# Attention passes: 800 tile gathers into a ring and 900 copies from it, in place of 900 gathers

## The chip, the cores and the metric

The kernel runs on one core of one Trainium2 chip. The metric is the device time of one execution in microseconds (us), and the median of the runs is compared.

## The reference, cut to what is computed

A graph of 3125 nodes with 64 features each and 100000 edges sorted by destination goes through two GATv2 attention layers (8 heads, then 4), a layer norm, a neighbour sum with a small dense network, and a second layer norm. The change touches only the two attention layers. One of them is, cut to what matters:

```
xl = (x @ Wl).reshape(N, heads, Dh)
xr = (x @ Wr).reshape(N, heads, Dh)
e = jax.nn.leaky_relu(xl[src] + xr[dst], NEG_SLOPE)
logits = jnp.einsum('ehd,hd->eh', e, att)
m = jax.ops.segment_max(logits, dst, num_segments=n_nodes)
a = jnp.exp(logits - m[dst])
denom = jax.ops.segment_sum(a, dst, num_segments=n_nodes)
out = jax.ops.segment_sum(alpha[:, :, None] * xl[src], dst, num_segments=n_nodes)
```

For every edge the row of its source node (64 floats, 256 bytes) has to be fetched: `x[src]`.

## The kernel before, in words

The edges are cut into 800 **tiles** of 125 edges (`G`, `T`). A **unit** is a tile seen against one window of 32 destination nodes; a tile that crosses a window's border is in two units, so that 800 tiles give 897 units, padded to 900 (`UT`). Twenty units make a **count** (`CU`), and a layer's pass over the edges is 45 counts (`NCH`), each worked in five steps q = 0 to 4 (`NQ`) of four units. The tensors' names begin with L1_ in layer 1 and L2_ in layer 2; the profile leaves the digit out.

In a pass (`edge_pass`) the engines run these streams, in each of which the order is that of the code:

- GpSimd (POOL) issues one indirect DMA per unit (L826, ahead of the pass L533), which gathers 125 rows of `x` from HBM into a buffer of the count, `xs`. There are 6 such buffers in layer 1 and 9 in layer 2. It waits only for the buffer (`v_ready`: the sums of the count that used it last).
- SyncE (SP) loads for each unit its window's node rows, `xw` (L547; 3 buffers). The window's number is read into a register by one load for each unit (L545). Behind the 20 loads it issues in order: the list of windows of the next count (L539), `dlb` of this count (L862), `lim` of the last one (L845), and the store of maxima `me` (L869).
- TensorE (PE) opens each step of a count by turning the four units' rows (L888, function `turn`), which at q = 0 waits for the gathers, for `xw` and for `oht`. Then come the projection (L901), the logits (L910, L913), and for an earlier count the turned maxima and weights (L923) and the weighted sums (L952).
- VectorE (DVE) does everything in one in-order stream. `spread_hot` of count c+1 (L1071), which makes `oht` out of `dlb`, stands in the body of count c at q = 1, n = 3. All of count c's later work on DVE stands behind it.
- ScalarE (ACT) copies, applies relu and exp, and stores the sums.

Layer 1 has four projections of each step, layer 2 has two. Ahead of each pass stands a block that prepares the layer (`prepare_layer`), in layer 2 also one for the neighbour sum's tables (`count_tables`). The blocks are separated by barriers over all engines, and the gathers of the first counts (`AHEAD` = 1 and 4) are issued in them. In the setup (`build_staircase`) the lists are made: `gidx` is the tile of each unit, `srcu` and `src_idx` its 125 source indices.

Of the kernel before, what the change touches and what calls it, by code (L numbers as in the profile page):

```python
# [112 lines left out]
def fixed(c):  # L113
    return Turn(c)
# [94 lines left out]
def build_staircase(nc, k, a, ctx0, x0):  # L209
# [4 lines left out]
    k.src_idx = sbuf(nc, ctx0, "src_idx", [T, UT], I32)  # L214
# [7 lines left out]
    with ExitStack() as ctx:  # L222
# [51 lines left out]
        ps = [psum(nc, ctx, f"ps_setup{i}") for i in range(4)]  # L274
        s = {n: k.setup.enter_context(nc.semaphore("st_" + n)) for n in (
            "load", "iota", "ident0", "ident", "dve", "dve2", "dve3", "store", "transposed", "pad",
            "load2", "sides", "last", "upto2", "node", "keys", "lim", "x_pad", "dloc", "dl0", "row0", "pre", "pre_dma", "below0", "below")}
# [5 lines left out]
        with nc.Block() as block:  # L283
            @block.sync
            def _(sp):
                sp.dma_start(dg[:], a["dst"].rearrange("(p k e) -> p k e", k=KT, e=T)).then_inc(s["load"], 16)
                ld = Dma(sp, s["load2"])
                ld.start(x0[:], a["x"].rearrange("(p t) d -> p t d", t=NT))
                sp.wait_ge(s["pad"], 2)
# [15 lines left out]
                xs.wait()  # L305

# [35 lines left out]
        with nc.Block() as block:  # L342
# [10 lines left out]

            @block.gpsimd
            def _(pool):
                pool.wait_ge(s["dve2"], 2 * NB + 2)
                for b in range(NB):
                    pool.indirect_dma_start(srcu[:, b * T:(b + 1) * T], None, a["src"].rearrange("(g e) -> g e", e=T),
                                            bass.IndirectOffsetOnAxis(gidx[:, b:b + 1], 0)).then_inc(s["gather"], 16)
                    pool.indirect_dma_start(dstu[:, b * T:(b + 1) * T], None, a["dst"].rearrange("(g e) -> g e", e=T),  # L360
                                            bass.IndirectOffsetOnAxis(gidx[:, b:b + 1], 0)).then_inc(s["gather"], 16)
                pool.wait_ge(s["gather"], 32 * NB)
# [22 lines left out]
        with nc.Block() as block:  # L385
            @block.vector
            def _(dve):
# [33 lines left out]
                dve.wait_ge(s["transposed"], 2 * NB)  # L421
                link(dve.tensor_copy(k.src_idx[:, 0:5 * BLK], ps[0][0:T, 0:5 * BLK]))
                link(dve.tensor_copy(k.src_idx[:, 5 * BLK:UT], ps[1][0:T, 0:4 * BLK]))
# [50 lines left out]
            def _(pe):  # L474
                pe.wait_ge(s["dve3"], NB + 2)
                for b in range(NB):
                    c = slice((b % 5) * BLK, (b % 5 + 1) * BLK)
                    pe.transpose(ps[b // 5][0:T, c], srcf[:, b * T:(b + 1) * T],
                                 k.ident[0:BLK, 0:BLK]).then_inc(s["transposed"], 1)
# [47 lines left out]

def fetch_rows(k, pool, lay, u0, u1):  # L530

    for u in range(u0, u1):
        pool.indirect_dma_start(lay.xs[u // CU][:, u % CU, 0:D], None, lay.x_rows,  # L533
# [1523 lines left out]
```

## Time and profile before

| | |
|---|---|
| runs, median of 3 | 4058.42 us (4051.95 to 4059.17) |
| profiled execution, its span | 4048.7 us |
| of it layer 1's pass, from the first turn | 198.5 to about 1810 us |
| layer 2's pass, POOL's gathers | 2085.0 to 3413.3 us |
| PE busy, POOL busy over the span | 3293.6 us, 2796.9 us |
| TensorE's granted clock, mean of the span | 0.90 of full |

The profiled execution's own time is the span from its first to its last instruction; the median of the runs is 9.7 us above it, which lies around the span. A busy time is the sum of instructions' durations. An idle time in square brackets stands before an instruction and names what ended it. DMA-issuing instructions of SP and ACT (SPq, ACTq) and the loads of registers aren't counted as busy.

### The profile page before, as it was taken

How to read it: one execution, taken by the hardware profiler on the slowest of the kernel's cores; microseconds unless marked ns; L12 is line 12 of the kernel's file. 1: busy time of each engine (PE TensorE's matmuls, PEld its weight loads, DVE VectorE, ACT ScalarE, POOL GpSimd, SP SyncE). 2: the span in 40 equal slices, each digit the busy share in tenths (PEclk: the TensorE clock that was granted, in tenths of full speed). 3: DMA queues.
4: the chain of work that ended last, by engine and by line, in shares of the span. 5: the costliest groups of instructions: out<-in, count | busy, mean ns of one | idle time of the engine just before them, and what ended most of it. 6: DMA issues, size and time to landing. Idle time of an engine off the chain costs nothing. (4 is left out here: it accounts for less than half of the span.)

```text
span 4048.7 us, 76266 instructions
## 1 busy us (share of the span) xinstructions
PE 3293.6 (81%) x24199; PEld 2204.4 (54%) x24199; DVE 2807.3 (69%) x6887; ACT 1717.6 (42%) x3696; POOL 2796.9 (69%) x2157
## 2 busy tenths in 40 slices
PE   0399999999999999996339977777777777568986
PEld 0246666666666666674226655554455555346763
DVE  3558888888888888886537755565555555579972
ACT  3254444444444444432215433333333333147861
POOL 4488888888777777505678888888888885537630
PEclk9999999999999999986669988888888888569997
DMA  2233343343333333323114433333333332211210
GB/s 58 51 65 80 86 88 86 86 89 85 80 87 86 86 85 88 75 54 83 48 36 79 91 74 67 68 69 67 67 68 73 69 68 48 52 26 40 44 34 28
DMA packets 607173, 274.68 MB, mean 68 GB/s; under 512 B 445801, under 2 KB 568077, under 8 KB 606260
## 3 DMA queue, kind: packets, MB, share of 16 engines
q1 hardware_dynamic: 261848, 102.14, 11.7%
q0 software_dynamic: 107328, 77.78, 11.1%
q10 hardware_dynamic: 237600, 89.88, 9.1%
q8 instruction: 198, 3.24, 0.3%
q14 instruction: 199, 1.63, 0.1%
HBM read 161.25 MB, written 105.94 MB: 66 GB/s over the span
## 5 line engine op out<-in xcount | busy, mean ns | idle before, releaser
L901 PE MATMUL L_e_ps_z<-L_e_xT,L_w_abs 128*128 128x500 f32 x2700 | 1501.4, 642 | 0.0
L826 POOL DMA_INDIRECT L_e_xs<-in_x_dram,src_idx x880 | 1193.1, 1356 | 335.4 <-issue 261.4
L826 POOL DMA_INDIRECT L_e_xs<-x_d,src_idx x820 | 1079.7, 1317 | 253.3 <-issue 249.8
L952 PEld LDWEIGHTS L_e_ps_v<-L_e_xs,L_e_p 125*128 125x128 f32 x5400 | 860.0, 204 | 628.3 <-issue 569.6
L996 ACT ACTIVATE L_e_rl<-L_e_ps_z 128x500 f32<-128x500 f32 x1350 | 793.0, 587 | 883.0 <-PE L_e_ps_z L901 883.0
L952 PE MATMUL L_e_ps_v<-L_e_xs,L_e_p 125*128 125x65 f32 x5400 | 796.2, 274 | 11.1 <-DVE L_e_acc L1180 9.4
L1180 DVE SCALAR_TENSOR_TENSOR L_e_acc<-L_e_acc,L_e_row,L_e_ps_v 128x130 f32<-128x130 f32 (+1 forms) x1440 | 448.5, 311 | 424.1 <-PE L_e_ps_v L952 281.4
L888 PE MATMUL L_e_ps_x<-ident,L_e_xs 125*64 125x125 f32 x1800 | 288.7, 285 | 310.7 <-DMA L_e_xs<-x_d,src_idx 251.8
L989 ACT ACTIVATE L_e_xT<-L_e_ps_x 128x500 f32<-128x500 f32 x450 | 264.3, 587 | 619.3 <-PE L_e_ps_x L891 590.4
L901 PEld LDWEIGHTS L_e_ps_z<-L_e_xT,L_w_abs 128*128 128x128 f32 x2700 | 427.4, 198 | 77.8 <-issue 24.3
L1163 DVE TENSOR_TENSOR L_e_p<-L_e_ohc,L_e_ae 125x640 f32<-125x640 f32 x540 | 427.1, 818 | 0.0
L888 PEld LDWEIGHTS L_e_ps_x<-ident,L_e_xs 125*64 125x64 f32 x1800 | 188.7, 120 | 354.4 <-DMA L_e_xs<-x_d,src_idx 261.0
L1185 DVE SCALAR_TENSOR_TENSOR L_e_acc<-L_e_acc,L_e_keep,L_e_ps_v 128x65 f32<-128x65 f32 x540 | 134.8, 277 | 314.4 <-PE L_e_ps_v L952 311.9
L1091 DVE SCALAR_TENSOR_TENSOR L_e_f<-L_e_rl,L_sign 128x500 f32<-128x500 f32 x450 | 326.2, 725 | 21.7 <-ACT L_e_rl L996 21.4
L1091 DVE SCALAR_TENSOR_TENSOR L_e_f<-L_e_rl,L_sign,L_e_f 128x500 f32<-128x500 f32 x450 | 329.8, 733 | 4.2 <-ACT L_e_rl L996 0.8
L1655 POOL DMA_INDIRECT g_xs<-x_d,src_idx x168 | 209.1, 1244 | 139.9 <-POOLq L1604 58.9
L1770 ACT ACTIVATE g_cnt<-g_ps_c 125x400 bf16<-125x400 f32 x512 | 257.5, 504 | 63.7 <-PE g_ps_c L1706 54.6
L1800 DVE TENSOR_SCALAR g_ohk<-t_keys_n,t_key_of 125x200 bf16<-125x200 bf16 x1024 | 237.3, 322 | 1.0 <-PE g_ps_c L1706 1.0
L1706 PE MATMUL g_ps_c<-g_ohk,g_ohr 125*128 125x200 bf16 x1024 | 176.7, 255 | 48.2 <-DVE g_ohk L1800 44.5
L1716 PE MATMUL g_ps_s<-g_x,g_cnt 125*128 125x192 bf16 x1600 | 195.8, 248 | 10.4 <-DVE g_sums L1806 10.3
L910 PE MATMUL L_e_ps_l<-L_e_xT,L_w_lin 128*32 128x125 f32 x3600 | 189.9, 283 | 10.5 <-DVE L_e_f L1091 10.5
L891 PE MATMUL L_e_ps_x<-L_e_oht,L_e_xw 96*64 96x125 bf16 x1800 | 193.4, 233 | 0.0
(304 smaller groups left out, 3620.2 us busy)
## 6 DMA issues: line engine op xcount, KB each, us to landing
L_v_d<-L_e_acc ACTq DMA_DIRECT2D x225, 260.0 KB
L_e_dlb<-dloc_d SPq DMA_DIRECT2D x90, 468.8 KB, 4.9
L_v_d<-L_e_acc ACTq DMA_DIRECT2D x225, 130.0 KB
L_e_xw<-x_d SPq DMA_DIRECT2D x1800, 12.0 KB
L_e_xs<-in_x_dram,src_idx POOLq DMA_INDIRECT x900
L_e_xs<-x_d,src_idx POOLq DMA_INDIRECT x900
L_e_lim<-limits_d SPq DMA_DIRECT2D x180, 39.1 KB
L_max_d<-L_e_me SPq DMA_DIRECT2D x45, 78.1 KB
```

The costliest lines, as they stand in the source:

```text
L826: pool.indirect_dma_start(xs[c.slot(XR)][:, n, 0:D], None, lay.x_rows, bass.IndirectOffsetOnAxis(k.src_idx[:, u:u + 1], 0)).then_inc(gath[ ...
L888: pe.transpose(ps[0:D, j * T:(j + 1) * T], xs[r][:, n, 0:D], k.ident[0:T, 0:T])
L901: pe.matmul(ps_z[part % ZR][:, 0:QT], lay.w_abs[:, part * 128:(part + 1) * 128], xT[q][:], start=True, stop=True).then_inc(s["z_ready"], 1)
L952: ins = pe.matmul(ps_v[u // 2 % 2][:, u % 2 * VX + v * XW:u % 2 * VX + (v + 1) * XW], p[st % 3][:, u % NQ, v, :, :].rearrange("e n h -> e ...
L989: act.activation(xT[q][:], ps_x[(c.slot(2) * NQ + q) % 2][:, 0:QT], ACT.Copy).then_inc(s["xT_ready"], 1)
L996: act.activation(rl[n % NE][:], ps_z[part % ZR][:, 0:QT], ACT.Relu, scale=1.0 - SLOPE).then_inc(s["relu_done"], 1)
L1091: dve.scalar_tensor_tensor(out=f[g % 3][:], in0=rl[(C * g + part) % NE][:], scalar=lay.sign[:, part:part + 1], in1=rl[(C * g) % NE][:] if ...
L1163: ins = dve.tensor_tensor(p[n % 3][:, :, v, :, :], ohc[c.slot(2)][:, us, :].unsqueeze(3).to_broadcast([T, NQ, WN, HL]), ae[c.slot(2)][:, u ...
L1180: ins = dve.scalar_tensor_tensor(out=to, in0=prev, scalar=row[c.slot(2)][:, u:u + 1], in1=ps_v[u // 2 % 2][:, u % 2 * VX:(u % 2 + 1) * VX] ...
L1655: pool.indirect_dma_start(xs[p][:, j, :], None, table, bass.IndirectOffsetOnAxis(k.src_idx[:, u:u + 1], 0)).then_inc(gath[p], 16)
L1770: act.activation(cnt[i % CR][:, :, 2 * j:2 * j + 2, :], ps_c[n % 2][0:T, 0:2 * KEYS].rearrange("r (u t n) -> r t u n", u=2, n=EN), ACT.Cop ...
L1800: dve.tensor_scalar(ohk[v % KR][:], keys_n[:], key_of[:, v:v + 1], None, ALU.is_equal).then_inc(s["hot"], 1)
```

## The change

POOL no longer gathers for each unit. It gathers each of the 800 tiles once, in 50 groups of 16 (`NF`, `TF`), into a ring of 64 tiles in SBUF (`TR`; `tiles`). SP copies the rows of each unit out of the ring into `xs` by a plain DMA from SBUF to SBUF, 20 for each count, behind that count's `xw` loads and ahead of its `dlb`. Three semaphores tie the two: `fetched_to` (POOL tells that a group has landed, four gathers into the next group, or at a block's end at once), `copied` (SP tells that a count's copies have landed, once it has issued the next count's `xw` loads), and POOL's wait for `copied` before it overwrites a group's place. The counts that these waits need are worked out in the setup and read into registers. For this input, the groups that the counts 0 to 44 need are 1 to 8 for counts 0 to 7, 10 to 18 for 8 to 16, 20 to 28 for 17 to 25, 30 to 38 for 26 to 34, 40 to 47 for 35 to 42, and 49 for 43 and 44. `xs` has 6 buffers in both layers. The registers of 20 units are now loaded by one instruction (`listed`). `dlb` and `lim` have 2 buffers in layer 1 and 3 in layer 2 (`SLACK`). The setup gathers `srcu` for two of nine blocks only, turns the tiles' indices instead, and stores two more lists.

```diff
+TR = 64
+TF = 16
+NF = G // TF
+RF = TR // TF
+XR = 6
+SERVED = (1, 3)
+FETCHED = (2, 4)
...
+def counts(eng, name, places):
+    regs = [eng.alloc_register(f"{name}{n}") for n in range(places.shape[1])]
+    eng.load(regs, places)
+    return [(eng.snap(r, donate=True, min_val=0, max_val=63) & 63) + 1 for r in regs]
+def fetch_tiles(k, pool, lay, f0, f1):
+    for f in range(f0, f1):
+        if f >= RF:
+            if (f - RF) % 16 == 0:
+                copies = counts(pool, f"{lay.nm}reuse{f}_", k.reuse[0:1, f - RF:min(f + 16, f1) - RF])
+            pool.wait_ge(lay.copied, copies[(f - RF) % 16])
+            pool.sem_inc(lay.freed, 1)
+        for i in range(TF):
+            g = f * TF + i
+            pool.indirect_dma_start(lay.tiles[:, g % TR * D:(g % TR + 1) * D], None, lay.x_rows,
+                                    bass.IndirectOffsetOnAxis(k.src_tile[:, g:g + 1], 0)).then_inc(lay.gath[f % RF], 16)
+            if i == 3 and f > f0:
+                tiles_there(pool, lay, f - 1)
+    tiles_there(pool, lay, f1 - 1)
+def tiles_there(pool, lay, f):
+    pool.wait_ge(lay.gath[f % RF], 16 * TF * (f // RF + 1))
+    pool.sem_inc(lay.fetched_to, 1)
...
+def listed(sp, lay, c, row, top):
+    regs = [sp.alloc_register(f"{lay.nm}{row}_{c.number}_{n}") for n in range(CU)]
+    sp.load(regs, lay.lists[c.slot(2)][0:1, row, :])
+    return [sp.snap(r, donate=True, min_val=0, max_val=top) for r in regs]
 def load_windows(k, sp, lay, c):
-    for n in range(CU):
-        window = k.nc.values_load(lay.wins[c.slot(2)][0:1, n:n + 1], engines=[mybir.EngineType.SP], min_val=0, max_val=NW - 1,
...
+    for n, at in enumerate(listed(sp, lay, c, 0, (NW - 1) * WN * S3)):
+        sp.dma_start(lay.xw[c.slot(3)][:, n, :], bass.AP(k.x3_d.tensor, at,
...
+def rows_there(sp, lay, c):
+    sp.wait_ge(lay.ld_r[c.slot(XR)], c.uses(XR) * 16 * CU)
+    sp.sem_inc(lay.copied, 1)
+def load_rows(k, sp, lay, c):
+    places = listed(sp, lay, c, 1, (TR - 1) * D)
+    sp.wait_ge(lay.fetched_to, counts(sp, f"{lay.nm}need{c.number}_", lay.lists[c.slot(2)][0:1, 2, CU - 1:CU])[0])
+    for n, at in enumerate(places):
+        sp.dma_start(lay.xs[c.slot(XR)][:, n, 0:D], lay.tiles[:, bass.ds(at, D)]).then_inc(lay.ld_r[c.slot(XR)], 16)
+def serve(k, sp, lay, c):
+    sp.wait_ge(lay.ld_w[c.slot(2)], c.uses(2) * 16)
+    load_windows(k, sp, lay, c)
+    if c.after(1):
+        rows_there(sp, lay, c.back(1))
+    load_rows(k, sp, lay, c)
+    if c.back(-1).there():
+        list_units(k, sp, lay, c.back(-1))
...
                     if c.there():
-                        if c.after(3):
-                            sp.wait_ge(s["x_ready"], c.val(NQ, -2 * NQ))
-                        if c.after(1):
-                            sp.wait_ge(ld_w[c.slot(2)], c.uses(2) * 16)
-                            load_windows(k, sp, lay, c)
-                        if c.back(-1).there():
-                            list_windows(k, sp, lay, c.back(-1))
-                        if c.after(3):
-                            sp.wait_ge(s["oht_ready"], c.val(1, -2))
+                        if c.after(lay.served):
+                            if c.after(3):
+                                sp.wait_ge(s["x_ready"], c.val(NQ, -2 * NQ))
+                            if c.after(XR):
+                                sp.wait_ge(s["v_ready"], c.val(CU, CU * (1 - XR)))
+                            serve(k, sp, lay, c)
+                        if c.after(SLACK):
+                            sp.wait_ge(s["oht_ready"], c.val(1, 1 - SLACK))
                         sp.dma_start(dlb[r][:], ...
...
-                        pe.wait_ge(gath[r], c.uses(XR) * GB)
+                        pe.wait_ge(ld_r[r], c.uses(XR) * GB)
```

On POOL, in the middle of layer 1's pass, a count's gathers stood as these rows before. `v_ready` is PE's semaphore for the sums.

```order
L826 DMA L_e_xs<-in_x_dram,src_idx 125x64 [waits e_v_ready]
L826 DMA L_e_xs<-in_x_dram,src_idx 125x64 x19
L826 DMA L_e_xs<-in_x_dram,src_idx 125x64 [waits e_v_ready]
L826 DMA L_e_xs<-in_x_dram,src_idx 125x64 x19
L832 DMA L_node_max<-L_max_d,max_idx 125x8 [waits e_m_store1,e_m_store0]
```

At the same place stands now a group of 16, which waits first for SP's copies and at its fifth gather for the landing of the group before.

```order
L594 REGISTER_ALU x2
L598 DMA L_e_tiles<-in_x_dram,src_tile 125x64 [waits L1_e_copied]
L598 DMA L_e_tiles<-in_x_dram,src_tile 125x64 x3
L598 DMA L_e_tiles<-in_x_dram,src_tile 125x64 [waits L1_e_gath3]
L598 DMA L_e_tiles<-in_x_dram,src_tile 125x64 x11
```

POOL's wait has moved from PE's sums to SP's copies, and it falls every 16 gathers rather than every 20.

On SP, in layer 1's pass, one count's work was this before; between the first three rows and the rest stand 19 more such threes.

```order
L545 TENSOR_LOAD L_e_wins [waits L1_e_ld_w0,e_x_ready]
L547 ISA
L547 DMA L_e_xw<-x_d 96x64
...
L539 DMA L_e_wins<-win_d 1x20
L862 DMA L_e_dlb<-dloc_d 96x2500 [waits e_oht_ready]
L845 DMA L_e_lim<-limits_d 8x2x625 [waits e_falls_ready]
L845 DMA L_e_lim<-limits_d 8x2x625 x3
L869 DMA L_max_d<-L_e_me 125x160 [waits e_left]
```

Now it is this, with 20 pairs of the rows of L626 and 20 pairs of those of L641 (the first of these pairs carries the wait).

```order
L619 TENSOR_LOAD L_e_lists [waits L1_e_ld_w0,e_v_ready,e_x_ready]
L626 REGISTER_ALU
L626 DMA L_e_xw<-x_d 96x64
...
L619 TENSOR_LOAD L_e_lists [waits L1_e_ld_r5]
L584 TENSOR_LOAD L_e_lists
L639 REGISTER_ALU x2
L641 ISA [waits L1_e_fetched_to]
L641 DMA L_e_xs<-L_e_tiles 125x64
...
L613 DMA L_e_lists<-unit_d 1x3x20
L963 DMA L_e_dlb<-dloc_d 96x2500 [waits e_oht_ready]
L947 DMA L_e_lim<-limits_d 8x2x625 [waits e_falls_ready]
L947 DMA L_e_lim<-limits_d 8x2x625 x3
L970 DMA L_max_d<-L_e_me 125x160 [waits e_left]
```

`dlb`, `lim` and the store of maxima stand behind the wait for the gathers now (`fetched_to`), which SP did not have before.

## Rows read from the trace of the kernel before

**Rows 1.** The page: span and busy time of each engine.

```profile
span 4048.7 us, 76266 instructions
PE 3293.6 (81%) x24199; PEld 2204.4 (54%) x24199; DVE 2807.3 (69%) x6887; ACT 1717.6 (42%) x3696; POOL 2796.9 (69%) x2157
```

**Rows 2.** Windows: busy us of each engine in both passes, clock, DMA share, GB/s.

```profile
287.00:1738.00 1451.00, 1451.00 (x10417) 963.61 (x10415) 1208.10 (x2578) 716.49 (x1476) 1113.26 (x820) 1.00 0.38 84
2085.00:3414.00 1329.00, 1061.27 (x8252) 689.25 (x8252) 794.96 (x1890) 502.01 (x1127) 1079.20 (x820) 0.88 0.37 70
```

**Rows 3.** Line L888, 2300 to 3416: what its engines' idle time waited for.

```profile
  DMA L_e_xs<-x_d,src_idx: 499.5, 68
```

**Rows 4.** Tile xs: POOL's gathers in layer 2's pass, ns, first and last start.

```profile
L826 POOL DMA_INDIRECT L_e_xs<-x_d,src_idx x820: 1206/1212/3333, 2085.0 to 3413.3; - x164
```

**Rows 5.** Timeline, PE: turns that open counts 1 to 4 of layer 1.

```profile
226.34 0.62 PE L888 MATMUL L_e_ps_x<-ident,L_e_xs 125*64 125x125 f32 x4
256.56 1.04 PE L888 MATMUL L_e_ps_x<-ident,L_e_xs 125*64 125x125 f32 x4 [4.61 <-DMA L_e_xs<-in_x_dram,src_idx]
286.77 0.62 PE L888 MATMUL L_e_ps_x<-ident,L_e_xs 125*64 125x125 f32 x4 [0.92 <-DMA L_e_xs<-in_x_dram,src_idx]
322.16 0.51 PE L888 MATMUL L_e_ps_x<-ident,L_e_xs 125*64 125x125 f32 x3
```

**Rows 6.** Timeline: the load of dlb for count 1 and the DVE that waits for it.

```profile
210.58 0.32 SPq L862 DMA_DIRECT2D L_e_dlb<-dloc_d  x1
215.73 0.96 DVE L1071 TENSOR_SCALAR L_e_oht<-L_e_dlb,L_oht_node 96x2500 bf16<-96x2500 bf16 x1 [17.41 <-DMA L_e_dlb<-dloc_d]
```

**Rows 7.** Lines L545 and L547 on SP, ns of one, then one count of layer 2.

```profile
L545 SPq TENSOR_LOAD <-L_e_wins x1800: 260/269/962, 153.5 to 3357.8; - x180
L547 SPq FUSED_REGOPS  x1800: 37/37/51, 154.0 to 3358.1; - x180
L547 SPq MOVE L_e_xw<-x_d x1800: 29/29/38, 154.1 to 3358.2; - x180
L547 SPq DMA_DIRECT2D L_e_xw<-x_d x1800: 317/317/1682, 154.2 to 3358.3; - x180
2503.17 16.35 SPq L547 DMA_DIRECT2D L_e_xw<-x_d  x20
2522.18 1.28 SPq L845 DMA_DIRECT2D L_e_lim<-limits_d  x4
```

**Rows 8.** Timeline, POOL: last gathers ahead of each block's end, first of the next.

```profile
168.77 1.21 POOL L533 DMA_INDIRECT L_e_xs<-in_x_dram,src_idx  x1 [0.30 <-issue]
188.82 1.21 POOL L826 DMA_INDIRECT L_e_xs<-in_x_dram,src_idx  x1 [18.84 <-POOLq L606]
...
2060.59 1.21 POOL L533 DMA_INDIRECT L_e_xs<-x_d,src_idx  x1 [0.30 <-issue]
...
2080.29 1.21 POOL L533 DMA_INDIRECT L_e_xs<-x_d,src_idx  x1 [0.31 <-issue]
```

**Rows 9.** Timeline, setup: POOL's last gather of 18, SP's stores, DVE's next block.

```profile
36.87 0.29 SPq L150 DMA_DIRECT2D w_d<-wcol  x1
44.25 0.36 SPq L150 DMA_DIRECT2D wrow<-w_d  x1
59.48 1.01 POOL L360 DMA_INDIRECT dstu<-in_dst_dram,gidx  x1 [0.30 <-issue]
64.07 0.18 DVE L390 TENSOR_SCALAR tiles_upto<-tiles_upto 125x25 f32<-125x25 f32 x1 [27.02 <-PEq L342]
```

**Rows 10.** Timeline, PE in layer 2: two counts at full pace, and the last turn.

```profile
2252.55 0.59 PE L888 MATMUL L_e_ps_x<-ident,L_e_xs 125*64 125x125 f32 x4
2275.13 0.59 PE L888 MATMUL L_e_ps_x<-ident,L_e_xs 125*64 125x125 f32 x4
3416.33 1.04 PE L888 MATMUL L_e_ps_x<-ident,L_e_xs 125*64 125x125 f32 x4 [6.54 <-DMA L_e_xs<-x_d,src_idx]
```

**Rows 11.** The page: SP's DMA queue, packets, MB, share of 16 engines' span.

```profile
q1 hardware_dynamic: 261848, 102.14, 11.7%
```

More of the change, by code:

```diff
@@ L542, in load_windows @@
 def load_windows(k, sp, lay, c):
-    for n in range(CU):
-        window = k.nc.values_load(lay.wins[c.slot(2)][0:1, n:n + 1], engines=[mybir.EngineType.SP], min_val=0, max_val=NW - 1,
-                                  skip_runtime_bounds_check_because="win_idx is the least of a count's rest and NW - 1")
-        sp.dma_start(lay.xw[c.slot(3)][:, n, :], bass.AP(k.x3_d.tensor, window * (WN * S3),
+    for n, at in enumerate(listed(sp, lay, c, 0, (NW - 1) * WN * S3)):
+        sp.dma_start(lay.xw[c.slot(3)][:, n, :], bass.AP(k.x3_d.tensor, at,
@@ L571, in prepare_layer @@
     lay.xs = [sbuf(nc, ctx, f"{lay.nm}e_xs{r}", [T, CU, XW]) for r in range(XR)]
-    lay.gath = [semaphore(nc, k, f"{lay.nm}e_gath{r}") for r in range(XR)]
+    lay.tiles = sbuf(nc, ctx, lay.nm + "e_tiles", [T, TR * D])
+    lay.gath = [semaphore(nc, k, f"{lay.nm}e_gath{r}") for r in range(RF)]
+    lay.fetched_to = semaphore(nc, k, lay.nm + "e_fetched_to")
+    lay.copied = semaphore(nc, k, lay.nm + "e_copied")
+    lay.freed = semaphore(nc, k, lay.nm + "e_freed")
     lay.xw = [sbuf(nc, ctx, f"{lay.nm}e_xw{r}", [3 * WN, CU, D], BF16) for r in range(3)]
-    lay.wins = [sbuf(nc, ctx, f"{lay.nm}e_wins{r}", [1, CU], I32) for r in range(2)]
+    lay.lists = [sbuf(nc, ctx, f"{lay.nm}e_lists{r}", [1, 3, CU], I32) for r in range(2)]
+    lay.ld_r = [semaphore(nc, k, f"{lay.nm}e_ld_r{r}") for r in range(XR)]
     lay.ld_x = [semaphore(nc, k, f"{lay.nm}e_ld_x{r}") for r in range(3)]
@@ L634, in _ @@
                 pool.wait_ge(s["ones"], XR)
-                fetch_rows(k, pool, lay, 0, EARLY if lay.norm else lay.ahead * CU)
+                fetch_tiles(k, pool, lay, 0, 2)
             @block.vector
@@ L768, in edge_pass @@
         ph, nm = "e_", lay.nm + "e_"
-        dlb = [sbuf(nc, ctx, f"{nm}dlb{r}", [3 * WN, CU * T], BF16) for r in range(3)]
+        dlb = [sbuf(nc, ctx, f"{nm}dlb{r}", [3 * WN, CU * T], BF16) for r in range(SLACK)]
         oht = [sbuf(nc, ctx, f"{nm}oht{r}", [3 * WN, CU * T], BF16) for r in range(2)]
@@ L1495, in _ @@
                              allow_slow_non_contiguous=True).then_inc(s["load"], 16)
+                for c in range(1, lay.served):
+                    serve(k, sp, lay, fixed(c))
                 sp.wait_ge(s["load"], 48)
```

158 lines of the change are left out of this document (94 added, 64 removed).

## The prediction

> **What bounds the kernel now.** The page gives the size of things: a span of 4048.7 us in which no engine is busy throughout [rows 1]. So I cut it at the passes. In layer 1's pass PE is busy for 1451.0 of 1451 us at full clock. In layer 2's it has 1061.3 of 1329 us and a granted clock of 0.88 [rows 2]. The line that opens a count says what PE lacks there: 499.5 us of idle time, PE and its weight loads together, ended with the landing of `xs` [rows 3]. POOL issues 820 gathers from 2085.0 to 3413.3, one each 1.622 us, at a median of 1.21 us plus 0.30 of issue, the rest DVE's interference [rows 4]. Twenty are 32.4 us. PE alone needs 22.6 us for a count of layer 2 [rows 10]. So POOL's gathers bound layer 2 and PE bounds layer 1. In layer 1 the change can only cost; in layer 2 it can win.
>
> **The gathers.** In layer 2, 64 tiles are gathered ahead of the pass and 736 in it, against 820: 84 x 1.622 = **-136 us** [rows 4]. A count's share falls to 17.8 gathers, 28.8 us. Each of the 46 groups adds a wait, increments and two register operations on POOL. The nearest rows are register operations of 0.03 and 0.04 us and a load of 0.27 [rows 7]. Bounds are 0 and 0.5 us a group, and I take 0.2: **+10 us**.
>
> **The ring.** POOL may overwrite a group when its last count is copied and SP has issued the next count's windows. That is about 6.5 us (four gathers) + 7.7 + 2.5 + 10.4 (worked out below) = 27 us after the start of the group that follows the needed one. POOL comes to it two groups, 52 us, later, except where a count needs one group more than usual (counts 8, 17, 26, 35): there it has one group, 26 us, and stands still for a microsecond or two. I take **+9 us**, between 0 and 30.
>
> **SP.** One window cost 16.35/20 = 0.82 us: load 0.27, operation 0.04, move 0.03, DMA 0.32, gaps 0.16 [rows 7]. Without the load a DMA with its register work is 0.38 us at least, 0.55 at most (all gaps kept). No row shows a load of 20 registers; it lies between 0.27 us and 20 x 0.27 = 5.4. The list, `dlb`, `lim` and the maxima cost some 2.5 us (`lim` 1.28 of it). A count of SP is then 40 x 0.38 + 2.5 + 0.3 + 2 x load = 18.5 to 29 us, at 0.55 for each DMA up to 36. I take 0.38, since the gap is nearest to the load that has gone, and 2.7 us for a load, the middle: 23.5 us, under POOL's 28.8 and under layer 1's 35 (1451 us for some 41 counts) [rows 2, 7]. The copies of a count take 7.7 us, its windows 10.4. The Trainium skill ("Runtime: NRT & Kernel Launch", Instruction fetch mechanics) puts a bulk register load at about 200 ns for each register. By that rule a load is 4.0 us and SP's count 26 us, still under POOL's; no row here shows such a load.
>
> **What is late now.** `dlb` of count c stood ahead of everything that waits for gathers; now it stands behind the copies of c, and these behind the landing of c's last group, as SP's rows in the section on the change show. DVE needs it in the body of count c-1. The trace shows what follows: `dlb` of count 1 was issued at 210.58, DVE stood still for 17.41 us and went on at 215.73, and only then could PE finish the count and turn count 1, at 226.34 [rows 5, 6]. So from a landed group to the turn: copies 7.7 + list and issue 0.7 + landing 5.2 + the rest of the body, 10.6 in a body without sums and by layer 2's full pace about 16 us with them (0.7 of 22.6). In the middle of layer 2 this delay costs nothing, since POOL's rate decides and a body of 22.6 us fits between two groups (16 x 1.622 = 26.0). At both ends of a pass it is paid.
>
> *Layer 1, start* (times of before). The 20th gather starts at 168.77; 12 more at 1.65 us end at 190, landing 2.5, copies 7.7, block change 2: POOL's pass starts at 202.5 rather than 188.8 [rows 8]. Count 1 needs group 2, told after 20 gathers: 235.5. Its `dlb` is there at 249, turn 1 at 260 (before 226.3). Count 2 (16 gathers on): 262, `dlb` 275.5, the rest of its body about 17.5: turn 2 at 293. Turn 3 follows after the old 29.3 us, at 322, against 286.8 [rows 5]. From there PE's own work bounds again: **+35 us**. Bounds: +12, if only the gathers' delay counts (16 more minus what PE's first counts had to spare), and +50.
>
> *Layer 1, middle.* With two buffers `lim` of count c-1 waits for DVE in body c-1, and SP is tied one count behind PE. By the sum above `dlb` still lands some 10 us before DVE asks. I take 0; if SP's count were 36 us, this cover would be gone.
>
> *Setup.* Seven gathers fewer are -9.2 us, but SP now stores two lists after `wrow`, and the like store took 44.25 - 36.87 = 7.4 us: SP ends near 57 where POOL ended at 60.5 + 2 [rows 9]. **-6 us**, between -9 and 0.
>
> *Ahead of layer 2.* The first block ends 4 us later (32 gathers rather than 35, then landing and copies). The second had 45 gathers, the last started at 2080.29; the 32nd started at 2060.59 [rows 8]. With 4 us of shift, 3 of landing, 7.7 of copies and 2 of change the pass starts at 2077.5: **-7.5 us**.
>
> *Layer 2, end.* Counts 43 and 44 both need the last group, which lands 2 us after the last gather, at E. Count 43: `dlb` at E+15.5, turn at E+31.5. SP then needs 3 + 10.4 + 2.7 + 7.7 us for count 44, whose `dlb` is there at E+39, turn 44 at E+55. Before, the last turn came 1.8 us after the gather's end (3413.3 + 1.2; 3416.33) [rows 4, 10]: **+53 us**. Bounds +15 and +70. What follows that turn is unchanged.
>
> **Sum:** -6 + 35 - 7.5 - 136 + 10 + 9 + 53 = -42 us. The span goes from 4048.7 to 4007 and the runs' median, 9.7 above it, to **4017 us**.
>
> **Rivals.**
> A. *The lateness is mostly hidden*: the copies' chain costs no more than the gathers' delay, +15 at layer 1's start and +30 at layer 2's end. For it: DVE's stall of 17.41 us cost PE only a part. Against: in the last counts nothing else is left to do. 4017 - 20 - 23 = 3974 us.
> B. *DMA engines crowd the copies.* q1's packets took 0.117 x 16 x 4048.7 / 261848 = 29 ns each on average [rows 11], and the DMA share is 0.37 already [rows 2]. A count's copies are 2500 packets: 4.5 us over 16 engines, less than their issue; over five, 14.5 us, 7 more than assumed, which comes once at layer 1's start, once ahead of layer 2 and twice at its end: +25, 4042 us. The Trainium skill ("DMA: Bandwidth & Descriptors", Why a DMA increments its semaphore by 16 and not by 1) says that a DMA from SP runs on the largest number of engines up to 16 that divides the partitions, five for 125; that is this rival, and speaks against the change. No row here shows the spread.
> C. *SP becomes the bound* (the other side). Place: SP's stream in layer 2's pass, 40 DMAs, three loads and their order. It decides from 28.8 + 42/43 = 29.8 us a count; at 31 us the pass is 43 x 2.2 = 95 us longer than forecast: 4112 us. For it: the ends 29 and 36 of my own bounds, and DMAs of up to 1682 ns [rows 7]. Against: it needs nearly all of the unknown costs at their upper end.
> D. *The ring brakes POOL*: the change doesn't do what it says if POOL waits about 1 us for each us saved. It takes 20 us more delay of `copied` on every count, 4060 us.
>
> **Chances.** Forecast 0.50 (its own range 3992 to 4045), A 0.13, B 0.14, C 0.16, D 0.07. A change within 0.2%, 8 us, can't be told from none. Faster: 0.48 of the forecast, A, and 0.10 of B: 0.71. Same: 0.02 + 0.03 + 0.04 = 0.09. Slower: C, 0.03 of D and 0.01 of B: 0.20. The range reaches from A to a mild C: 3965 to 4090.
>
> **What would show it.** Right: in layer 2, 736 gathers at about 1.62 us with few waits for copies; PE's idle time ended by DVE's `oht` or sums rather than by gathers; DVE waits of many us for `dlb`, in the first counts of layer 1 and in every count of layer 2; SP idle for 5 us or more a count before L641; the last turn some 50 us after the last gather; layer 1's pass as long as before from turn 3 on. Wrong: SP never idle (C), copies that land more than 10 us after the last issue (B), idle time on POOL every group (D), or PE below full busy time in the middle of layer 1, which would add to everything.

## The result: slower, 4454 us

The changed kernel takes **4454.4 us** in the median (4434.4 to 4508.5, four runs), beside 4058.8 for the kernel before: ratio 1.0959, 95% interval 1.0924 to 1.0993. I had forecast 4017 and put 0.20 on slower. The profiled execution has a span of 4432.6 us, against 4048.7 in [rows 1].

One of the four runs, the one of 4508.5, was in the chip's slower state, and the ratio is formed from the other three.

How much slower depends on more than that. The kernels were timed in sets, each with runs of the kernel before beside them (the expectations below speak of a call). Before's median was 4039 to 4045 us in some sets and 4058 to 4086 in others; the changed kernel lost 5.1% in the first kind, which I call quiet, and 9.6% and 11.1% in the others. The record numbers the chips: 4, 6 and 0 in the quiet sets, 9, 9 and 0 in three of the others. The same number 0 stands beside 4044.8 and beside 4085.9, so the chip's number doesn't tell the two kinds apart. Every comparison of medians below stays within a set, or within quiet sets, and the two parts of the loss are explained apart. Of the kernel before there is one profile, from the first set, whose execution took 4052.0 us, 7 to 13 us more than the quiet medians of before. So a difference of a few us between its stages and those of a quiet run proves nothing.

### The profile page after: what moved, and what is told of

The parts are those of the page before. It is cut to its first block and busy times, and to the rows that moved or that the text cites. A ratio compares the mean times of both kernels' runs of the same rounds, so it can differ in the third digit from the quotient of the medians.

```text
span 4432.6 us, 78798 instructions
## 1 busy us (share of the span) xinstructions
PE 3487.8 (79%) x24200; PEld 2279.4 (51%) x24200; DVE 2813.8 (63%) x6896; ACT 1691.5 (38%) x3697; POOL 2511.8 (57%) x1947
## 3 DMA queue, kind: packets, MB, share of 16 engines
q1 hardware_dynamic: 498838, 160.20, 16.5%
## 5 line engine op out<-in xcount | busy, mean ns | idle before, releaser
L1002 PE MATMUL L_e_ps_z<-L_e_xT,L_w_abs 128*128 128x500 f32 x2700 | 1556.6, 662 | 119.6 <-issue 88.1
L598 POOL DMA_INDIRECT L_e_tiles<-in_x_dram,src_tile x800 | 1086.8, 1358 | 613.7 <-SPq L633 358.6
L598 POOL DMA_INDIRECT L_e_tiles<-x_d,src_tile x800 | 1038.4, 1298 | 529.0 <-SPq L633 264.8
L1053 PEld LDWEIGHTS L_e_ps_v<-L_e_xs,L_e_p 125*128 125x128 f32 x5400 | 883.9, 210 | 764.7 <-issue 660.0
L1053 PE MATMUL L_e_ps_v<-L_e_xs,L_e_p 125*128 125x65 f32 x5400 | 829.2, 281 | 107.0 <-DVE L_e_acc L1281 57.9
L1002 PEld LDWEIGHTS L_e_ps_z<-L_e_xT,L_w_abs 128*128 128x128 f32 x2700 | 441.2, 202 | 223.8 <-issue 145.9
L989 PE MATMUL L_e_ps_x<-ident,L_e_xs 125*64 125x125 f32 x1800 | 299.7, 287 | 104.3 <-issue 68.2
L1104 ACT ACTIVATE L_e_lg<-L_e_ps_l 128x125 f32<-128x125 f32 x450 | 124.6, 277 | 640.1 <-remote 446.1
L1172 DVE TENSOR_SCALAR L_e_oht<-L_e_dlb,L_oht_node 96x2500 bf16<-96x2500 bf16 x90 | 79.8, 887 | 324.1 <-DMA L_e_dlb<-dloc_d 265.5
L1014 PE MATMUL L_e_ps_l<-L_e_f,L_sign_sum 128*32 128x125 f32 x3600 | 216.8, 284 | 33.1 <-issue 32.4
```

Of the source, the lines that this page charges most:

```text
L598: pool.indirect_dma_start(lay.tiles[:, g % TR * D:(g % TR + 1) * D], None, lay.x_rows, bass.IndirectOffsetOnAxis(k.src_tile[:, g:g + 1], 0 ...
L989: pe.transpose(ps[0:D, j * T:(j + 1) * T], xs[r][:, n, 0:D], k.ident[0:T, 0:T])
L1002: pe.matmul(ps_z[part % ZR][:, 0:QT], lay.w_abs[:, part * 128:(part + 1) * 128], xT[q][:], start=True, stop=True).then_inc(s["z_ready"], 1)
L1014: ins = pe.matmul(ps_l[32 * j:32 * j + 32, 0:T], lay.sign_sum[:], f[g % 3][:, j * T:(j + 1) * T], start=False, stop=True)
L1053: ins = pe.matmul(ps_v[u // 2 % 2][:, u % 2 * VX + v * XW:u % 2 * VX + (v + 1) * XW], p[st % 3][:, u % NQ, v, :, :].rearrange("e n h -> e ...
```

## The profile after

Below are lines of the page of the changed kernel: span, busy time by engine, TensorE's granted clock in 40 slices, and SyncE's DMA queue, which had 261848 packets and 11.7% in [rows 11].

```profile
span 4432.6 us, 78798 instructions
PE 3487.8 (79%) x24200; PEld 2279.4 (51%) x24200; DVE 2813.8 (63%) x6896; ACT 1691.5 (38%) x3697; POOL 2511.8 (57%) x1947
PEclk9889998999999999986667888778878888759997
q1 hardware_dynamic: 498838, 160.20, 16.5%
```

The next rows are SyncE's: the row copies (L641), the register load of a count's list (L619) and the list's own transfer (L613, here from the quiet run of the same kernel, introduced below). Each shows min/median/max in ns.

```profile
L641 SPq DMA_DIRECT2D L_e_xs<-L_e_tiles x1800: 3/705/906, 185.3 to 3779.8; - x180
L619 SPq TENSOR_LOAD <-L_e_lists x180: 750/1439/2966, 148.2 to 3762.0; - x180
```

```profile
L613 SPq DMA_DIRECT2D L_e_lists<-unit_d x90: 680/690/750, 130.5 to 3567.3; - x90
```

A copy's issue takes 705 ns, the window's load 317 [rows 7]. And this is the timeline of SyncE in layer 2 of the changed kernel, one count and the start of the next:

```profile
2916.32 9.80 SPq L626 DMA_DIRECT2D L_e_xw<-x_d  x20
2928.35 16.96 SPq L641 DMA_DIRECT2D L_e_xs<-L_e_tiles  x20
2945.35 0.68 SPq L613 DMA_DIRECT2D L_e_lists<-unit_d  x1
2946.07 0.42 SPq L963 DMA_DIRECT2D L_e_dlb<-dloc_d  x1
2946.54 1.33 SPq L947 DMA_DIRECT2D L_e_lim<-limits_d  x4
2950.34 10.48 SPq L626 DMA_DIRECT2D L_e_xw<-x_d  x20
```

From window to window it is 34.0 us here, 35.0 in the next count; in the quiet run the mean of 36 counts between 2300 and 3560 us is 34.2. In it the queue is idle for no more than its own register work: 20 copies take 17 us, where I had 7.7, 20 windows 10 to 11, two register loads some 3.

The other engines' waits in a quiet set show who suffers. This is the chain of waits of GpSimd, SyncE, VectorE and PE, 2300 to 3600 us, in a quiet run of the changed kernel (engine, line, released by: us, times, longest):

```profile
POOL L_e_tiles L598 <- SPq L633: 208.7, 25, 10.8
...
SPq L641 <- POOLq L608: 3.9, 6, 0.9
...
DVE L_e_oht L1172 <- DMA L_e_dlb<-dloc_d: 504.5, 38, 16.9
...
PE L_e_ps_v L1053 <- DVE L_e_acc L1281: 336.1, 38, 12.4
```

SyncE waits for nobody (3.9 us in 1300), which was the forecast's own sign of rival C. GpSimd waits for its copies, VectorE for the one-hot's load that stands in its queue, PE for VectorE. The gathers that bounded this layer [rows 3, 4] are now the ones that are held up.

The turns on PE, five in a count, cut the span in parts. For each kernel: the line that turns the rows, its first and last start in layer 1, then in layer 2. The first pair is the kernel before's, the second the changed kernel's first profile, the third a quiet run of it.

```profile
L888 PE MATMUL L_e_ps_x<-ident,L_e_xs x900: 267/270/417, 198.5 to 1766.8; 125*64 125x125 f32 x180
L888 PE MATMUL L_e_ps_x<-ident,L_e_xs x900: 267/270/418, 2095.2 to 3437.3; 125*64 125x125 f32 x180
```

```profile
L989 PE MATMUL L_e_ps_x<-ident,L_e_xs x900: 267/270/417, 211.5 to 1950.5; 125*64 125x125 f32 x180
L989 PE MATMUL L_e_ps_x<-ident,L_e_xs x900: 267/270/417, 2292.0 to 3814.0; 125*64 125x125 f32 x180
```

```profile
L989 PE MATMUL L_e_ps_x<-ident,L_e_xs x900: 267/270/417, 212.6 to 1816.7; 125*64 125x125 f32 x180
L989 PE MATMUL L_e_ps_x<-ident,L_e_xs x900: 267/270/417, 2158.9 to 3635.6; 125*64 125x125 f32 x180
```

| us | before | changed, first profile | changed, quiet |
|---|---|---|---|
| up to the first turn | 198.5 | 211.5 | 212.6 |
| turns of layer 1 | 1568.3 | 1739.0 | 1604.1 |
| between the layers | 328.4 | 341.5 | 342.2 |
| turns of layer 2 | 1342.1 | 1522.0 | 1476.7 |
| behind the last turn | 611.4 | 618.6 | 615.7 |

The quiet run's span is 202.6 us longer than before's: 14.1 to the first turn, 35.8 in layer 1, 13.8 between, 134.6 in layer 2 and 4.3 behind. The first profile adds 134.9 us in layer 1 and 45.3 in layer 2.

## The experiments

My theory after the result: SyncE's issuing is the bound of layer 2, since a copy's issue costs more than twice the row that I priced it by. The rivals were the copies' traffic, the ring, and the place of the one-hot's load behind the copies. The first four runs shared a quiet set (before 4039.3 us).

**What an issue costs.** Six forms of the copy in turn, by the count's number:

```
-        sp.dma_start(lay.xs[..][:, n, 0:D], lay.tiles[:, bass.ds(at, D)])
+        # count % 6: 125, 128, 96 or 64 partitions of the ring at `at`;
+        # 125 rows of x_rows (DRAM) at `at`; 125 partitions of ident, fixed
```

> The changed kernel with six forms of the row copy, one after the other by the count's number (about 8 of the 45 counts of each pass each): 125 partitions from the ring at an address in a register (as in the changed kernel, 705 ns median on SyncE), the same with 128 partitions, with 96, with 64, 125 rows taken from the node table in DRAM at the same register, and 125 partitions from a fixed SBUF address. It reads wrong or partial rows in five of the six, so only the price of an issue counts. If the price goes by the number of partitions: about 720 ns at 128, 540 at 96, 360 at 64, and 705 from DRAM and from the fixed address. If it goes by a count that 16 does not divide: about 317 ns (the window's load, 96 partitions) at 128, 96 and 64, and 705 at the three others. If it goes by SBUF as the source: 600 to 720 at all SBUF forms, 317 to 400 from DRAM. If it is the register: the fixed address alone falls to 320 to 400.

Measured, ns of one issue (L645 125 partitions, L647 128, L649 96, L651 from DRAM, L653 a fixed address, L655 64):

```profile
L645 SPq DMA_DIRECT2D L_e_xs<-L_e_tiles x320: 705/706/915, 192.8 to 3385.8; - x160
L647 SPq DMA_DIRECT2D L_e_xs<-L_e_tiles x320: 492/519/1743, 237.6 to 3415.8; - x160
L649 SPq DMA_DIRECT2D L_e_xs<-L_e_tiles x320: 532/532/1828, 266.7 to 3447.4; - x160
L651 SPq DMA_DIRECT2D L_e_xs<-in_x_dram x140: 262/263/541, 296.0 to 1558.9; - x140
L653 SPq DMA_DIRECT2D L_e_xs<-ident x280: 684/685/873, 319.0 to 3322.6; - x140
L655 SPq DMA_DIRECT2D L_e_xs<-L_e_tiles x280: 496/515/1609, 351.5 to 3352.3; - x140
```

Neither the register nor the size sets the price. A transfer from SBUF to SBUF costs some 515 ns whether it has 64 or 128 partitions, and 706 at 125. The same 125 rows from DRAM cost 263. No expectation had both parts; the one on SBUF as the source came nearest. Why 125 partitions are dearer than 128 isn't shown. This run copies wrong or partial rows in five of the six forms, so only the prices count.

**Ten copies of twenty.**

```
-    for n, at in enumerate(places):
+    for n, at in list(enumerate(places))[::2]:
```

> The changed kernel with the 10 even copies of each count alone (the odd units read a constant). If SyncE's issuing is the bound, its count falls from 34.8 us by 8.5 to 26.3 and is under the gathers' count of 28.8 and PE's 34.7 of layer 1: the span returns to what the forecast had, 4017 to 4110 us. If it is the ring that holds GpSimd, or the clock, or turns that depend on the lists: it stays within 60 us of 4454.

Measured: 4007.2 us, ratio 0.9912 (0.9896 to 0.9929), below the expected range's lower end by 10 us. Layer 2's turns take 1287.2 us, 55 less than before. This kernel computes wrong values, since half of the units read a constant, and it leaves out half of the copies' traffic as well as half of their issues. The ring, the lists, the counters and the order are all in place, and with SyncE relieved the forecast's -42 us comes out as -32. SyncE now waits for the gathers, 2300 to 3300 us:

```profile
SPq L641 <- POOLq L608: 109.9, 31, 26.9
```

**The copies on ScalarE**, four behind each of its steps, all work whole:

```
+                    for n in range(Q * q, Q * q + Q):
+                        act.dma_start(xs[b.slot(XR)][:, n, 0:D], lay.tiles[:, bass.ds(at[n], D)])...
```

> All 20 copies of a count are kept, with the same bytes, but ScalarE issues them, four behind each of its five steps, from the third count on. If SyncE's issuing is the bound: SyncE's count falls to about 18 us, ScalarE's rises from 13 to 16 us busy by 14 to 17 us and stays under 32.4 in layer 2; 4030 to 4150 us, of which what lies above 4060 is layer 1, where ScalarE is nearly full. If the copies' traffic on the DMA engines, or the ring, is what costs: it stays at 4400 or more.

Measured: 4422.0 us, ratio 1.0951 (1.0927 to 1.0975). By the total the rival had won; the parts say otherwise. Layer 2's turns take 1266.0 us, 76 fewer than before, with all the traffic; layer 1's 1988.4, 420 more. This is ScalarE's timeline there:

```profile
908.74 3.23 ACTq L1163 DMA_DIRECT2D L_e_xs<-L_e_tiles  x4
912.02 0.27 ACT L1106 ACTIVATE L_e_lg<-L_e_ps_l 128x125 f32<-128x125 f32 x1 [3.17 <-issue]
916.86 3.23 ACTq L1163 DMA_DIRECT2D L_e_xs<-L_e_tiles  x4
920.13 0.28 ACT L1106 ACTIVATE L_e_lg<-L_e_ps_l 128x125 f32<-128x125 f32 x1 [3.16 <-issue]
```

Four issues keep ScalarE from its next copy for 3.2 us in each step of layer 1, where PE has no time to spare. So traffic isn't the cause in layer 2. (This edit also frees the one-hot's load from its place behind the copies; the run with that load ahead, below, prices that.) My estimate for layer 1 took ScalarE's busy time and not its place in PE's loop.

**Before, with 20 unread copies per count on SyncE**, from the fifth count on:

```
+                            for n in range(20):
+                                sp.dma_start(spare[:, n, :], k.ident[0:T, 0:D]).then_inc(extra, 16)
```

> The kernel before, with all its 900 gathers per pass and its single register loads, in which SyncE also issues 20 copies of 125 partitions from SBUF into a spare tile per count, behind the load of the one-hot's destinations. Nothing reads them. If SyncE's issuing is the bound: its count goes from about 20 to about 37 us, 4.6 over the 32.4 of layer 2 and 2 over the 35 of layer 1, and the time from 4058 to about 4300 us (4200 to 4400). If the copies are cheap where no ring and no waits hang on them: 4058, within 20 us.

Measured: 4204.5 us, ratio 1.0406 (1.0389 to 1.0423). Layer 2's turns take 1496.2 us (+154), layer 1's 1566.3 (-2). The timeline of SyncE in layer 2:

```profile
2913.81 16.55 SPq L547 DMA_DIRECT2D L_e_xw<-x_d  x20
2930.77 0.32 SPq L864 DMA_DIRECT2D L_e_dlb<-dloc_d  x1
2931.13 14.57 SPq L869 DMA_DIRECT2D L_e_spare<-ident  x20
2948.45 17.02 SPq L547 DMA_DIRECT2D L_e_xw<-x_d  x20
```

A count is 34.6 us, over the 32.4 of the gathers and under PE's 35 of layer 1. I expected 37 and 4300. SyncE waits for nobody here either, in 2300 to 3400 us:

```profile
SPq L545 <- PE L_e_ps_x L899: 1.0, 2, 0.6
```

Issues alone, with no ring and no other engine that waits for the copies, make a loss of the right kind.

**Three edits of the changed kernel**, in a second quiet set (before 4044.9). Copies over all 128 partitions:

```
-    lay.tiles = sbuf(nc, ctx, lay.nm + "e_tiles", [T, TR * D])
+    lay.tiles = sbuf(nc, ctx, lay.nm + "e_tiles", [128, TR * D])   # xs too
```

> The changed kernel with ring and unit buffers of 128 partitions and every copy over all 128 (partitions 125 to 127 hold zeros that nobody reads): the work is whole, only the form of the copy differs. If SyncE's issuing is the bound, the time follows the price of an issue: 705 to 515 ns saves 20 x 0.19 = 3.8 us of a count of 34.8, so 31.0 in layer 2, and layer 1 falls from 36.2 to its own 35: layer 2's turns end 44 x 3.8 = 167 us sooner, layer 1's about 150, together 4130 to 4230 us. If not the issue but the landing or the lists set the pace: 4400 or more.

Measured: 4093.1 us, 1.0112 (1.0097 to 1.0127). Layer 2's turns fall to 1348.5 and a count of SyncE to 31.8 (a window starts at 2925.14, the next at 2956.96); the mean of 32 counts is 31.1. That is 6 us above before's turns, where rival C put the threshold at 29.8 us a count.

The one-hot's load issued ahead of windows and copies:

```
+                        sp.dma_start(dlb[r][:], ...).then_inc(ld_d[r], 16)
                         if c.after(lay.served):
                             ...
                             serve(k, sp, lay, c)
-                        sp.dma_start(dlb[r][:], ...).then_inc(ld_d[r], 16)
```

> The changed kernel in which SyncE issues the one-hot's load ahead of the windows and copies of its count and not behind them. SyncE issues as much as before. If its rate is the bound, the time stays at 4454 within 40 us: only the delay within a count moves. If what costs is that the one-hot (and VectorE, 265.5 us of waits on it) stands behind 17 us of copies: 4300 us or less.

Measured: 4213.5 us, 1.0417 (1.0401 to 1.0433). Against 4454 I first read this as 240 us for the place of one load. That was a comparison across sets, and wrong, as the repeated runs below show. Beside the changed kernel of another quiet set (4252.2 us) it is 39 us.

The copies from DRAM (GpSimd stores each group of 16 tiles):

```
+    pool.dma_start(lay.tiles_d[f], lay.tiles[:, f % RF * TF * D:(f % RF + 1) * TF * D])...
-        sp.dma_start(lay.xs[c.slot(XR)][:, n, 0:D], lay.tiles[:, bass.ds(at, D)])
+        sp.dma_start(lay.xs[..][:, n, 0:D], bass.AP(lay.tiles_d.tensor, at, [[TF * D, T], [1, D]]))
```

> GpSimd gathers each tile once into the ring, as in the changed kernel, and stores each group of 16 tiles with one transfer to a table in DRAM; SyncE takes the units' rows from there at an address in a register. Nobody has to wait until the ring is copied. All the work is whole; the copies' traffic is larger than in the changed kernel, only the source is another. If the issue from an SBUF source is the cause (705 ns, and 262 from DRAM): SyncE's count is 34.8 - 17.1 + 20 x 0.40 = 25.7 us, under both bounds; layer 1 as before the change, layer 2 at the gathers' 28.8 and 1 to 2 for the store: 3990 to 4080 us. If copies in themselves cost (transfers, semaphores, the 20-register loads): 4350 or more.

Measured: 4056.5 us, 1.0025 (1.0015 to 1.0035). Nine tenths of the loss is gone with the same 900 copies per layer, and with more traffic; in this form GpSimd no longer waits for SyncE's copies either. Their issue is 264 ns:

```profile
L646 SPq DMA_DIRECT2D L_e_xs<-L_tiles_d x1800: 260/264/2494, 191.9 to 3414.8; - x180
```

Layer 2's turns take 1319.0 us: 23 won, and given back ahead of them (35.5 us later at layer 2's first turn).

**Two that should have won.** Layer 1 as before the change and layer 2 with the ring and ScalarE's copies; and the changed kernel with both 128 partitions and the load ahead. Both fell in a set with before at 4059.8.

```
-    if not c.after(lay.by_act):
+    if lay.norm and not c.after(lay.by_act):     # layer 1: fetch_rows, as before
```

> Layer 1 as before the change (a gather per unit, three slots for the one-hot's load); layer 2 with the ring, its copies issued by ScalarE as in the run where ScalarE issues them. By the stages: 198.5 us to the first turn and 1568.3 of turns as before, 328 to 341 between the layers, 1266 of turns in layer 2 as that run showed (1342 before), 611 to 618 behind them: 3972 to 4000 us, ratio 0.985 to 0.99. If the short layer 2 of that run came from its slow layer 1 (a clock rested by it), layer 2 takes 1300 or more and the time is 4025 or more.

> The changed kernel with both edits of the earlier runs: copies of 128 partitions, and the one-hot's load issued ahead of them. If the two remove different losses in layer 2 (3.8 us of issue in each count; the waits of VectorE on the one-hot): the SyncE count there falls from 34.0 to 30.5, 4060 to 4080 us. If both removed one and the same loss: 4093 as with 128 partitions alone.

Measured: 4151.6 us (1.0223, 1.0188 to 1.0257) and 4161.2 (1.0282, 1.0242 to 1.0323). Both missed. Layer 2's turns took 1407.3 in the first, where the sum had 1266. The expectation's other branch asked for 1300 or more: the 1266 would then belong to a run whose layer 1 had been slow. The kind of set is the other possible reason, and no run separates them.

**The same kernels again, to test the set itself** (before 4085.9):

> The changed kernel as it is, beside the three edits on one and the same chip, since the medians of before differ from chip to chip (4039, 4045, 4059 and 4060 so far). If the chip plays no part: ratio 1.095 to its before, 4425 to 4460. If part of the loss comes from how late transfers land on some chips: between 4200 and 4400 here where before takes about 4040.

> The one-hot's load ahead of the copies once more, beside the changed kernel on the same chip. If the place of the load in SyncE's queue cost 5 per cent, it is 200 us or more under the changed kernel of this call; if the chip did it, the two are within 60 us.

> Copies of 128 partitions once more, beside the changed kernel on the same chip. If the issue's price sets the pace: at least 200 us under the changed kernel of this call wherever it runs; if the chip did it, within 60 us.

Measured: 4550.9 (1.1106), 4523.4 (1.1076) and 4338.1 (1.0598, 1.0563 to 1.0634). Side by side, the load's place is worth 27 us, which the two intervals (1.1048 to 1.1165 and 1.1026 to 1.1126) don't tell from none, and the 128 partitions 213. In layer 1's turns the three are alike: 1813, 1827 and 1816 us. The last is from an execution 64 us above its kernel's median; even if all 64 lay in layer 1, 1752 would be left beside 1588.6 in the quiet set. So most of layer 1's loss in this set is not SyncE's rate. In the set at 4059.8 the kernel with both edits had 1647.9.

**A quiet set again** (before 4044.8):

> The changed kernel as the yardstick of this call. Layer 1's turns took 1739 us in its first profile and 1813 in the second, 1568 before the change; layer 2's 1522 and 1549, 1342 before. If layer 1's loss belongs to the chip it runs on, it lies anywhere from 1586 to 1820 here; layer 2 stays at 1500 to 1550 on each chip, since it goes by SyncE's issues.

> The copies with DRAM as their source, on the same chip as the changed kernel. If the stalls of layer 1 (engines that stand while no release is shown) come from the copies' traffic whatever the source: layer 1 stays within 40 us of the changed kernel's, and the whole lies at 1.04 to 1.07 times before where that takes 1739 or more. If they come from SBUF as the source, or from SyncE's long issues: layer 1 returns to 1570 to 1590 us and the whole to 1.00 to 1.01 times before.

> The kernel before with 20 unread copies per count, on the same chip. SyncE's issuing is the same as in the changed kernel, and nobody waits for the copies. If issuing and traffic alone make the stalls: layer 1 goes up with the changed kernel's (over 1650 us where that has 1739), 1.07 or more in all. If it takes the ring, the lists or the waits of the change: layer 1 stays at 1566 to 1585 and the ratio at 1.04.

> Ten of the twenty copies, on the same chip. If the stalls grow with the copies: layer 1 lies halfway between 1568 and the changed kernel's. If they need SyncE to be near its limit: 1570 to 1600, on a slow chip too. Layer 2 at 1290 to 1340 either way.

Measured: 4252.2 us for the changed kernel, 1.0515 (1.0494 to 1.0536); from DRAM 4062.8, 1.0047; before with 20 copies 4212.9, 1.0419; half of the copies 4011.8, 0.992. Layer 1's turns: 1604, 1587, 1571 and 1577. The set was quiet, so it could not tell what makes the stalls of layer 1; it gives the changed kernel's loss without them.

**Is there a faster form?** The kernel with the old layer 1 and ScalarE's copies in layer 2 once more, and one whose copies in layer 2 are shared by SyncE and ScalarE:

```
-    for n, at in enumerate(places):
+    for n, at in list(enumerate(places))[::2 if c.after(lay.by_act) else 1]:   # odd n on ScalarE
```

> Layer 1 with the old gathers, layer 2 with the ring and ScalarE's copies, once more, since its first run met medians of before at 4060. If before takes about 4040 here: 3972 to 4000 us by the sum of the stages (layer 2's turns at 1266, 1342 before), ratio 0.985 to 0.99. Where before takes 4060 or more: 4130 to 4180 again.

> The same, with the even copies of layer 2 issued by SyncE and the odd ones by ScalarE, two behind each of its steps. SyncE's count there is 34.0 - 8.5 = 25.5 us and under the 28.8 of the gathers, ScalarE stands still for 1.6 us a step and not 3.2. If the gathers set layer 2's pace: 1270 to 1290 us of turns as with half of the copies, 3985 to 4010 us in all where before takes about 4040, ratio 0.985 to 0.993, and less than the other edit loses where before takes 4060. If two issuing engines that wait for each other's copies cost: over 4045.

Measured: 4143.4 (1.0202, 1.0171 to 1.0234) and 4205.1 (1.0354, 1.0304 to 1.0403), before at 4057.8. Layer 2's turns took 1393.2 and 1479.2 us. Neither beats the kernel before in such a set, and no quiet set came for them. The sum of parts from quiet runs for the first, 198.5 + 1568.3 + 341 + 1266 + 615 = 3989 us, is an estimate and stays one; its 1266 was not seen behind a fast layer 1.

## Why the prediction was wrong

**What bounds the kernel before** stood. With half of the copies the gathers bound layer 2 again, and the time falls below before's.

**The step that failed is "SP"**: "A count of SP is then 40 x 0.38 + 2.5 + 0.3 + 2 x load", 23.5 us taken, 36 at most. It measured 34 to 35. The step took the price of a copy's issue from the wrong row. Twenty copies took 16.7 to 17.0 us and not 7.7: I priced a transfer from SBUF to SBUF by the row of one from DRAM to SBUF [rows 7], and even my upper end of 0.55 us was under the 0.84 that it takes. That is +9.2 us. The windows took 9.8 and 10.5 us where 7.7 was taken (+2 to +3), the list's transfer 0.69 instead of 0.3. The two register loads took 1.44 us each, not 2.7 (-2.5). Together, with +3, 23.5 + 9.2 + 3 + 0.4 - 2.5 = 33.6 us. That the count stayed under my 36 is luck: that sum had 5.4 us for each register load, which made room for the copies. The Trainium skill's 200 ns for each register ("Runtime: NRT & Kernel Launch", Instruction fetch mechanics) would make 4.0 us of a load of 20; the measured 1.44 us, 72 ns for each, decides for these loads, whose list lies in SBUF.

**Rival C was the right one, at 0.16**. Its slope of 43 counts puts the quiet run's 34.2 us at 4112 + 3.2 x 43 = 4250 us; its median is 4252. That it fits so well is in part luck: up to turn 3 of layer 1 the run lost 14 us more than forecast, between the layers 21 more, and layer 2's turns are some 33 us shorter than the slope makes them. Rival C speaks of layer 2 alone, and the 4454 of the result lie 200 us above it; 134.9 us of the first profile's excess over the quiet one are layer 1's, and their cause stays open (below). Its counter-argument, that "nearly all of the unknown costs" must be at their upper end, was wrong: one of them beyond its bound was enough. That one term turned the forecast gain into a loss. The 9.7 us that I put around the span were mostly the spread between runs: the profiled execution took 4052.0 us in all, the median run 4058.4.

**The gathers, the ring and the POOL groups** were right: 55 us less in layer 2's turns with half of the copies, where -136 + 10 + 9 + 53 makes -64.

**Layer 1's start**: +35 forecast, with the setup's -6 it is +29. In the quiet run turn 3 is at 330.1, beside 286.8 in [rows 5] and 322 forecast: +43. **Its middle**, taken as 0, cost 7 us more there, and its cover was as thin as the text said ("if SP's count were 36 us, this cover would be gone"): SyncE's count is 35.5 us there in the mean, VectorE waits 116.4 us for the load in 300 to 1700 us, PE 5 us. In the first profile, whose turn 3 is at 337.6, it cost 126 us more (below).

**Setup and ahead of layer 2**: -6 and -7.5 forecast. In the quiet run the first turn came 14.1 us later and the gap between the layers grew by 13.8. Ahead of layer 2 three counts of copies have to be issued, at 17 us each; what the setup alone gained was not taken apart.

**Layer 2's end**: +53 after the last gather forecast. The quiet run has its last count's first turn at 3617.2 and its last gather at 3539.0: 78 us, beside 3 before, so +75, with copies of 17 us in the chain twice.

**Rival B** fell: with all the traffic and the issues on ScalarE layer 2 was faster than before. Its sign was a landing of more than 10 us after the last issue. In the run with the one-hot's load ahead PE waits for the copies themselves, so that a turn's start shows it:

```profile
2713.46 16.66 SPq L641 DMA_DIRECT2D L_e_xs<-L_e_tiles  x20
2731.57 1.04 PE L989 MATMUL L_e_ps_x<-ident,L_e_xs 125*64 125x125 f32 x4 [8.53 <-DMA L_e_xs<-L_e_tiles]
```

The last issue ends at 2730.12 and PE goes on at 2731.57, 1.5 us later. **Rival D** fell too: GpSimd waits 208.7 us for copies, but because SyncE is late with them; with half of the copies the same wait is 2.7 us in 2300 to 3300 us. **Rival A** had +15 at layer 1's start and +30 at layer 2's end; with all copies it was +43 and +75. In the two runs with half of the copies, whose 8.4 us a count are near the 7.7 that I had taken, turn 3 comes 18 and 21 us later and the last count's first turn 48 and 54 us: near A at the start, near the forecast at the end.

**What stays open: layer 1 outside quiet sets.** There several engines stand still with nothing shown that they wait for. This is the chain of waits of PE, 300 to 1700 us, in the first profile of the changed kernel; the quiet run has no such row:

```profile
PE L_e_ps_z L1002 <- issue: 46.5, 32, 8.1
PE L_e_ps_z L1002 <- ACT L_e_rl L1097: 25.0, 12, 5.8
```

And here the timeline of VectorE and PE at one such stall in it:

```profile
1290.22 0.46 DVE L1286 SCALAR_TENSOR_TENSOR L_e_acc<-L_e_acc,L_e_keep,L_e_ps_v 128x65 f32<-128x65 f32 x2
1304.73 0.35 DVE L1281 SCALAR_TENSOR_TENSOR L_e_acc<-L_e_acc,L_e_row,L_e_ps_v 128x130 f32<-128x130 f32 x1 [12.58 <-issue]
...
1299.67 2.04 PE L1002 MATMUL L_e_ps_z<-L_e_xT,L_w_abs 128*128 128x500 f32 x2 [8.06 <-issue]
1303.85 2.04 PE L1002 MATMUL L_e_ps_z<-L_e_xT,L_w_abs 128*128 128x500 f32 x2 [1.40 <-issue]
```

PE comes back with two matmuls in 2.04 us where it took 1.06 to 1.11 before: the granted clock is 0.50 of full from 1299.5 to 1302, the 1.2 GHz level, and was 1.00 from 1280 to 1290, ahead of 8.06 us of standing. The window 300 to 1000 has 0.96 in place of 1.00 in [rows 2]. The stall costs twice. SyncE shows it too: the windows' register moves of 29 ns take up to 711 ns in this profile, 42 in the quiet one. q1's packets take the same time in both: 0.165 x 16 x 4432.6 / 498838 = 23.5 ns, and 0.174 x 16 x 4251.3 / 498838 = 23.7. So it isn't slower transfers on this queue. Instructions that come late would look like this, but no row shows that, and whether the copies provoke the long stalls or the changed kernel only lacks the slack to hide it is not settled: before, with 20 copies, was never run in such a set. Two observations narrow it. The profile of before, from the same set as this one, has moves of at most 38 ns. The two kernels with the old layer 1, in the sets at 4059.8 and 4057.8, have moves of up to 607 and 712 ns there, without a copy in that layer, yet PE stands without a shown wait for only 3.5 and 5.5 us and the turns take 1580.6 and 1581.8 us. So late moves don't need the copies, and there they came with turns only 12 to 14 us longer.

## What to carry to other kernels

Price a DMA issue by a row of the same kind, both sides and the partitions, not by the nearest row in the queue; where none exists, the upper bound has to be far wider, and a queue that then comes near the bound is the forecast's weak point. Work taken off one engine at 1.6 us a gather is not won if another must issue one instruction for each unit: count its whole cycle first. And compare variants only beside runs of the same reference: the place of one load looked like 240 us across sets and was 27 to 39.

## What the hardware showed unexpectedly

- A transfer's issue on SyncE took 263 ns from DRAM to SBUF (125 partitions of 256 bytes), 515 to 532 from SBUF to SBUF at 64, 96 or 128 partitions, 706 at 125; on ScalarE the last took 732.
- An issue from SBUF to DRAM stays cheap: the maxima's store, also 125 partitions and no smaller than a copy (39 or 78 KB against 31), takes 0.26 us before and 0.30 after in the median.
- In the count shown above, PE went on with the copied rows 1.5 us after the last of 20 issues, at 125 partitions.
- A bulk load of 20 registers from SBUF takes 1.44 us in the median, one of a single register 0.27.
- The changed kernel, whose SyncE queue is at its limit, varied by 299 us between three sets (4252.2 to 4550.9) in which the kernel before varied by 41.
